# Attention with an image prompt on one core: the image prompt's scores as eight more columns of the last keys' round of maxima

## Chip, cores and metric

One core of a Trainium2 chip runs the whole program. The metric is the device time of one execution in microseconds (us); a result is the median of several executions. All arithmetic is fp32; where a matmul reads fp32r, its operands were split into two parts first, so that the product of the parts keeps fp32's accuracy.

## The reference, cut to what matters

```python
B, S, D, C, HEADS, TEXT, IPT = 8, 512, 320, 512, 20, 1593, 8   # head size 16
text, ip_h = ctx[:, :TEXT], ctx[:, TEXT:]
q = split_heads(x @ w_q)
out_text = softmax(q @ split_heads(text @ w_k).T / 4) @ split_heads(text @ w_v)
out_ip = softmax(q @ split_heads(ip_h @ w_k_ip).T / 4 + mask_ip) @ split_heads(ip_h @ w_v_ip)
out = merge(out_text + out_ip) @ w_out + b_out + x
```

Each of 8 batches has 512 queries and 20 heads of 16. A head attends to 1593 text keys and, in a softmax of its own, to 8 image-prompt (IP) keys under a mask.

## The kernel before

**Groups.** Four heads make a group, so a batch has 5 groups (`NG`) and the program 40. A group's two *stacks* stand at partitions 0 and 64 (`SIDES`): each holds K or Q of two heads in 48 rows, high part, high part and low part of fp32r, so one matmul of depth 48 multiplies exactly. K comes from TensorE in 400-column pieces, is copied from PSUM by ScalarE, split in two parts by GpSimd (`split_k`), stored to HBM by SyncE and loaded into a slot of `k_stack` (a ring of 3 groups).

**Two passes.** Scores are computed twice. First, with queries on the partitions, for their maxima: *rounds* 1 to 16 of a group are three 128x512 matmuls each (`max_tile`, line 699), reduced by VectorE as two banks and then one (lines 1040 and 1042). *Round 0* (`max_rest`, line 710) takes the last 64 keys, of which seven are keys again as padding: 16 matmuls of 64 columns into banks 0 and 1 of `max_bank`, and one reduce of 1024 elements (line 1033). The maxima go through a small matmul with the identity (`negative_piece`, line 618), a ScalarE copy and a DMA into two rows of the Q stack. Second, with keys on the partitions, scores minus maximum (`exp_tile`, line 747, and 751 for the tail), ScalarE's exp (line 935), and the product with V (`pv_tile`, line 763).

**The order.** Everything in the steady state is written out by hand in *visits*: 17 (`v` = 0 to 16) for each group `g`. A visit has two tiles of a round of maxima, three tiles of exp, the round's third tile, mostly one PV tile, and a turn of some other piece from a table, `work_plan` ("Q", "K", "V", "OUT", "IP", the transposes "TA" and "TB" of the IP probabilities, the small products "WA" and "WB"). The rounds run ahead of the exps by a group and three visits: round 0 of group n stands in visit 14 of group n-2, after the exp tiles, and is followed there by the negative piece and a PV tile. Visit 15 begins with two tiles of round 1, which wait for `max_taken`, the semaphore that the last reduce before them counts.

**The image prompt.** `ip_keys` makes K of the IP tokens of all batches once, at the start, twice over two halves of partitions; `own_k` (GpSimd, line 1220) spreads it into a block-diagonal `kip_own` per batch. `ip_piece` (line 559) multiplies a group's whole `q_full` with it, 8 matmuls of 64 columns into the work bank (the trace records each fp32 matmul twice), and `ip_scale` (line 1021) copies them scaled to `s_ip`, two VectorE instructions. The pieces stand at (g, v) = (0, 16), (1, 16), (2, 1), (3, 14), (4, 14), and two at the start. `ip_softmax` has six VectorE steps of a batch, at visits 3, 5, 6, 9, 10, 11 of group 2, with one exp of ScalarE at visit 8.

At the start (`PRO_PLAN`) pieces run without exps; from round 1 of group 0 on each has rounds beside it.

Of the kernel before, what the change touches and what calls it, by code (L numbers as in the profile page):

```python
# [29 lines left out]
VW = DH + 1  # L30

# [36 lines left out]
def work_plan(first, last):  # L68
# [19 lines left out]
    put(0, ("IP", 2), 1, (16, 1))  # L88
# [8 lines left out]
    put(1, ("IP", 3), 1, (16, 1))  # L97
    put(2, ("Q", 4), 3, (0, 3))
    put(2, ("IP", 4), 1, (1, 1))
# [10 lines left out]
    if not last:  # L110
# [11 lines left out]
        put(3, ("IP", 5), 1, (14, 1))  # L122
# [6 lines left out]
        put(4, ("IP", 6), 1, (14, 1))  # L129
# [13 lines left out]
SOFTMAX_AT = (3, 5, 6, 9, 10, 11)  # L143
# [20 lines left out]
PRO_PLAN += [(p, ALL, 0) for p in (("V", 0), ("V", 1), ("KIP",), ("V", 2), ("IP", 0))] + [(("Q", 1), (0, 3, 3), 0)]  # L164
TWO_PLACES = len(PRO_PLAN)
PRO_PLAN += [(("VIP",), ALL, 1), (("IP", 1), ALL, 1)]
PRO_PLAN += [(("V", t), half, 1) for t in range(3, V_FIRST - 1) for half in HALVES]
# [33 lines left out]
def cross_attention(nc, x, x_t, ctx_t, ctx_ip_t, boxes, grid, own_k_rows, own_v_rows, ident, w_q, w_k, w_v, w_k_ip, w_v_ip,  # L201
# [3 lines left out]
    scratch_r = nc.dram_tensor("scratch_r", (GH, S), FP32, kind="Internal").ap()  # L205

    ctx = ExitStack()
    with ctx:
# [14 lines left out]
        own_k_sb = sb("own_k_sb", [128, 8])  # L223
# [17 lines left out]
        k_stack = sb("k_stack", [128, RING, GH // SIDES, KEYS])  # L241
# [18 lines left out]
        kip = sb("kip", [128, NG, B * IPT])  # L260
        vip = sb("vip", [128, 3, B * IPT])
        kip_own = sb("kip_own", [128, NG, 8, IPT])
# [9 lines left out]
        ctx_ip = early[:, 2 * CT * D:2 * CT * D + CT * B * IPT].rearrange("p (c n) -> p c n", c=CT)  # L272

# [49 lines left out]
        kip_ready = sem("kip_ready")  # L323
# [54 lines left out]
        def _(sp):  # L378
# [21 lines left out]
            def load_k(n):  # L400
                sp.wait_ge(k_stored, (n + 1) * 32)
                slot = n % RING
                for side in range(SIDES):
                    for block, part in enumerate(BLOCKS):
                        row = side * SIDE + block * DH
                        sp.dma_start(k_stack[row:row + DH, slot, :, :], k_side(n, side)[part]).then_inc(stack_loaded[slot], 16)
# [9 lines left out]
            def load_first_k(c):  # L416

                sp.wait_ge(k_stored, 32)
                for side in range(SIDES):
                    for block, part in enumerate(BLOCKS):  # L420
                        row = side * SIDE + block * DH
                        sp.dma_start(k_stack[row:row + DH, 0, c, :], k_side(0, side)[part][:, c, :])\
                          .then_inc(stack_loaded[0] if c else head_loaded, 16)

# [42 lines left out]
            sp.wait_ge(stack_cleared, 4)  # L467
# [4 lines left out]
            load_tail(0)  # L472
            store_k(1)
            store_q(1)
            load_k(1)
# [47 lines left out]
        def _(pe):  # L523
# [29 lines left out]
            def ip_piece(g, q_number, kip_count, place=work_bank):  # L553

                pe.wait_ge(work_empty, q_number + 1)
                pe.wait_ge(kip_ready, kip_count)
                for n in range(2):
                    for at, rows in strips(128):
                        last = nc.tensor.matmul(place[at:at + rows, n * 64:(n + 1) * 64],  # L559
                                                q_full[:, n * 128 + at:n * 128 + at + rows],  # L560
                                                kip_own[:, g % NG, :, :].rearrange("p h t -> p (h t)"), start=True, stop=True)
                last.then_inc(work_full, 1)

# [57 lines left out]
            def work(b, piece, turn, first, last):  # L621
# [10 lines left out]
                elif kind == "IP":  # L632
                    ip_piece(piece[1], number(("Q", piece[1])), b + (2 if piece[1] >= NG else 1))
# [41 lines left out]
            def begin_round(n, r):  # L675
# [9 lines left out]
                if taken > 0:  # L685
                    pe.wait_ge(max_taken, taken)

# [80 lines left out]
            def ip_keys(place):  # L768

                for g in range(NG):  # L770
                    for half in range(2):
                        for ct in range(CT):
                            last = nc.tensor.matmul(place[half * GR:(half + 1) * GR, g * 64:(g + 1) * 64],
                                                    wk_ip[:, ct, g * GR:(g + 1) * GR], ctx_ip[:, ct, :],
                                                    start=(ct == 0), stop=(ct == CT - 1))
# [11 lines left out]
            for piece, turn, beside in PRO_PLAN:  # L787
# [17 lines left out]
                elif piece[0] == "IP":  # L805
                    ip_piece(piece[1], PRO_ORDER["Q", piece[1]], 1, place)
# [6 lines left out]
                else:  # L813
                    pe.wait_ge(cleared, 9)
                    pe.wait_ge(consts_loaded, 80)
# [57 lines left out]
        def _(act):  # L873
# [70 lines left out]
            for piece in PRO:  # L944
# [6 lines left out]
                elif piece[0] == "KIP":  # L951
                    act.wait_ge(work_full, number + 1)
                    copy(kip[:, :, :].rearrange("p g n -> p (g n)"), place[:, 0:D]).then_inc(work_empty, 1)
# [4 lines left out]
                elif piece[0] == "IP":  # L958
                    act.wait_ge(work_full, number + 1)
                    src = place[:, 0:128].rearrange("p (n f m) -> p n f m", n=2, f=2)  # L960
                    for half in range(2):
# [395 lines left out]
```

## Time and profile before

| | |
|---|---|
| three runs, median | 1882.86 us (1878.38 to 1886.68) |
| the profiled execution: its time, its span | 1878.19 us, 1876.3 us |
| TensorE busy | 1838.2 us, 98% |
| VectorE busy | 1327.8 us, 71% |
| ScalarE busy | 1202.4 us, 64% |
| GpSimd busy | 379.6 us, 20% |
| DMA share of 16 engines, all queues | 43.9% |

A busy TensorE in this table is an engine with a matmul in flight by the records; a matmul that waits between two others of its kind shows in the timeline only. Times of the profiled execution are given from the start of its span. In the trace "PE" is a matmul and "PEld" its weights' load. The batch in the middle of the span from which most rows below come is the third: its group 1 ends at about 616 us, group 2 at about 662, group 3 at about 706.

### The profile page before, as it was taken

To read this page: it belongs to the slowest core of one execution; us is meant where nothing else is said; L and a number is where in the kernel's file an instruction comes from. 1 tells how busy PE (TensorE), PEld (TensorE's weight loads), DVE (VectorE), ACT (ScalarE), POOL (GpSimd) and SP (SyncE) were. 2 spreads that over 40 slices of the span, in tenths; PEclk is the share of its full clock that TensorE was granted. 3 is DMA by queue.
4 is the path that set the end of the run, shared out by engine and by line. 5 is a ranking of instruction groups with operands and counts; after the bars stand their busy time and mean duration, and the time that the engine had idled before them with its cause. 6 is when DMAs were issued, how large, how long until landed. Compare 5 with 4: busy or idle time off the path is not lost.

```text
span 1876.3 us, 43039 instructions
## 1 busy us (share of the span) xinstructions
PE 1838.2 (98%) x17984; PEld 743.5 (40%) x17984; DVE 1327.8 (71%) x1673; ACT 1202.4 (64%) x2368; POOL 379.6 (20%) x475
## 2 busy tenths in 40 slices
PE   8999999999999999999999999999999999999997
PEld 3333344433444334443443434434344443444332
DVE  5778767686767767677666777667776677676861
ACT  1277666666666666666666666666666666666774
POOL 5112212212112211122211211112121212121000
PEclk9999999999999999999999999999999999999998
DMA  8546334353445444364443643436334363343400
GB/s 233 87 87 157 71 70 101 74 145 71 81 87 135 85 87 86 71 158 84 81 89 70 155 87 70 90 71 168 70 75 83 69 167 71 71 101 67 82 11 23
DMA packets 89011, 175.41 MB, mean 93 GB/s; under 512 B 36197, under 2 KB 60310, under 8 KB 85074
## 3 DMA queue, kind: packets, MB, share of 16 engines
q1 hardware_dynamic: 67826, 131.26, 36.4%
q0 software_dynamic: 18976, 40.10, 6.7%
q8 instruction: 141, 2.31, 0.6%
q10 hardware_dynamic: 2016, 1.31, 0.2%
q14 instruction: 52, 0.43, 0.1%
HBM read 117.57 MB, written 48.82 MB: 89 GB/s over the span
## 4 chain that ended last, share of the span: by engine, by line
PE 93%; DVE 4%; DMA 1%; issue 1%; SPq 1%; ACT 0%; ACTq 0%; POOLq 0%; POOL 0%
PE pv_bank L763 25%; PE max_bank L699 22%; PE work_bank L536 12%; PE work_bank L569 11%; PE exp_bank L747 10%; PE work_bank L585 3%; PE work_bank L547 3%; PE max_bank L710 2%; DVE tile_max L1033 2%; PE exp_bank L751 1%; DVE tile_max L1040 1%; PE work_bank L575 1%; DMA wq<-in_w_q 1%; PE work_bank L596 0%; PE work_bank L559 0%
## 5 line engine op out<-in xcount | busy, mean ns | idle before, releaser
L935 ACT ACTIVATE probs<-exp_bank 128x512 f32<-128x512 f32 x1896 | 995.5, 598 | 436.0 <-PE exp_bank L747 426.0
L1040 DVE TENSOR_REDUCE tile_max<-max_bank 128x2 f32<-128x1024 f32 x632 | 774.1, 1225 | 411.5 <-PE max_bank L699 406.3
L699 PE MATMUL max_bank<-k_stack,q_stack 48*128 48x512 f32 x1896 | 561.3, 464 | 14.4 <-DVE tile_max L1040 11.4
L763 PE MATMUL pv_bank<-probs,v_ones 128*17 128x512 f32 x3840 | 513.3, 599 | 0.1
L1042 DVE TENSOR_REDUCE tile_max<-max_bank 128x1 f32<-128x512 f32 x632 | 429.6, 680 | 0.7 <-PE max_bank L699 0.7
L747 PE MATMUL exp_bank<-q_stack,k_stack 50*128 50x512 f32 x1896 | 409.5, 401 | 2.0 <-DMA q_stack<-neg_rows 1.2
L699 PEld LDWEIGHTS max_bank<-k_stack,q_stack 48*128 48x128 f32 x1896 | 234.1, 184 | 397.9 <-issue 253.4
L536 PE MATMUL work_bank<-ctxt,wk 128*32 128x400 f32 x2528 | 253.5, 506 | 7.7 <-DMA wk<-in_w_k 5.5
L747 PEld LDWEIGHTS exp_bank<-q_stack,k_stack 50*128 50x128 f32 x1896 | 236.4, 187 | 42.5 <-ACT probs L935 29.0
L569 PE MATMUL work_bank<-wv,ctxt 128*32 128x320 f32 x3040 | 246.9, 434 | 0.0
L1233 POOL DMA_DIRECT2D sums<-o_sum x39 | 27.4, 703 | 681.3 <-ACT o_sum L875 681.3
L569 PEld LDWEIGHTS work_bank<-wv,ctxt 128*32 128x32 f32 x3040 | 91.9, 110 | 162.9 <-issue 103.6
L536 PEld LDWEIGHTS work_bank<-ctxt,wk 128*32 128x32 f32 x2528 | 74.9, 110 | 160.8 <-issue 137.6
L763 PEld LDWEIGHTS pv_bank<-probs,v_ones 128*17 128x17 f32 x3840 | 71.0, 95 | 159.9 <-issue 156.0
L1204 POOL TENSOR_TENSOR k_parts<-k_full,zero 128x400 fp32r<-128x400 f32 x80 | 68.6, 857 | 271.4 <-ACT k_full L875 270.9
L875 ACT ACTIVATE v_ones<-work_bank 128x320 f32<-128x320 f32 (+1 forms) x111 | 46.5, 419 | 77.9 <-PE work_bank L569 69.9
L1237 POOL DMA_DIRECT2D scratch_r<-recips x39 | 22.6, 579 | 316.9 <-DVE recips L1060 307.5
L1207 POOL TENSOR_TENSOR k_parts<-k_full,k_parts 128x400 fp32r<-128x400 f32 x80 | 83.3, 1042 | 6.4
L1033 DVE TENSOR_REDUCE tile_max<-max_bank 128x16 f32<-128x1024 f32 x40 | 49.0, 1226 | 37.1 <-PE max_bank L710 37.1
L935 ACT ACTIVATE probs_tail<-exp_bank 128x512 f32<-128x512 f32 x80 | 43.4, 595 | 47.6 <-PE exp_bank L751 47.6
L585 PE MATMUL work_bank<-wout,o_t 128*32 128x320 f32 (+1 forms) x896 | 71.0, 434 | 0.0
L1243 POOL TENSOR_TENSOR o_sum<-o_sum,r_wide 128x512 f32<-128x512 f32 x39 | 50.1, 1285 | 89.8 <-DMA r_wide<-scratch_r 89.8
(125 smaller groups left out, 903.6 us busy)
## 6 DMA issues: line engine op xcount, KB each, us to landing
k_stack<-scratch_k SPq DMA_DIRECT2D x234, 200.0 KB, 6.8
scratch_k<-k_parts SPq DMA_DIRECT2D x80, 400.0 KB, 4.7
ctxt<-in_ctx_t POOLq DMA_DIRECT2D x28, 800.0 KB, 11.2
q_stack<-scratch_q SPq DMA_DIRECT2D x240, 64.0 KB, 2.3
scratch_q<-q_parts SPq DMA_DIRECT2D x80, 128.0 KB, 5.4
r_wide<-scratch_r POOLq DMA_DIRECT2D x39, 256.0 KB, 5.2
xres<-in_x SPq DMA_DIRECT2D x8, 640.0 KB, 6.7
out<-xres SPq DMA_DIRECT2D x32, 160.0 KB, 1.9
```

The lines of the kernel that those rows point to most:

```text
L536: last = nc.tensor.matmul(place[half * GR + at:half * GR + at + rows, 0:CHUNK], wk[:, ct, dims:dims + rows], ctxt[:, ct, keys:keys + CHUNK ...
L569: last = nc.tensor.matmul(place[at:at + rows, 0:D], ctxt[:, ct, key:key + rows], wv[:, ct, :], start=(ct == 0), stop=(ct == CT - 1))
L585: last = nc.tensor.matmul(bank[at:at + rows, :], o_t[0:deep, k, t * 128 + at:t * 128 + at + rows], wout[0:deep, k, :], start=(k == 0), sto ...
L699: nc.tensor.matmul(round_place(n, r)[:, k, :], exact(q_stack[stack, slot, c, t * 128:(t + 1) * 128]), exact(k_stack[stack, slot, c, chunk ...
L747: nc.tensor.matmul(bank[:, :], exact(k_stack[stack, slot, c, kt * 128:(kt + 1) * 128]), exact(q_stack[stack, slot, c, :]), start=True, sto ...
L763: last = nc.tensor.matmul(pv_bank[h * 32:h * 32 + VW, :], v_ones[:, v_slot(b, kt), head * VW:(head + 1) * VW], p, start=(kt == 0), stop=(k ...
L935: nc.scalar.activation(dst, exp_place(group_no, at), ACT.Exp, scale=SCALE).then_inc(probs_ready, 1)
L1033: nc.vector.reduce_max(tile_max[:, :, CHUNKS, :].rearrange("p q s -> p s q"), max_bank[:, 0:SIDES, :].rearrange("p s (q k) -> p s q k", k= ...
L1040: nc.vector.reduce_max(flat[:, at:at + 2], place[:, 0:2, :], AX.X).then_inc(max_taken, 1)
L1042: nc.vector.reduce_max(flat[:, at + 2:at + 3], place[:, 2, :], AX.X).then_inc(max_third_taken, 1)
L1204: nc.gpsimd.tensor_tensor(exact(part[:, 0, :]), k_full[:, c, :], zero[:, :].to_broadcast([128, CHUNK]), ALU.add)\
L1207: nc.gpsimd.tensor_tensor(exact(part[:, 1, :]), k_full[:, c, :], part[:, 0, :], ALU.subtract).then_inc(k_split, 1)
```

## The change

The IP keys become columns of the K stack. `WITH_AGAIN` is 1594, `REST` 58, `WITH_IP` 66, `IN_BANK` 7: of the last keys only 58 stay (one key again instead of seven), the 8 IP keys stand behind them, and round 0 multiplies 66 columns. Seven of the 66-column blocks of a side fit in its bank; the eighth block of both sides goes to bank 2, so side 0 runs one block behind side 1 and the last matmul waits until the first is done (`third_begun`). The IP keys are made on one half of the partitions, split in two parts, stored and loaded to `ip_stack`, and GpSimd places a group's eight columns in its slot (`place_ip`). VectorE takes the maxima in two reduces and copies the IP scores with three more instructions before it counts `max_taken`. The IP pieces, `own_k`, `ip_scale` and the constant `own_k_rows` go; the softmax of the IP scores moves. The diff, cut to its core:

```diff
+WITH_AGAIN = TEXT + 1
+REST = WITH_AGAIN - KEYS // 512 * 512
+WITH_IP = REST + IPT
+IN_BANK = 512 // WITH_IP
...
-    put(0, ("IP", 2), 1, (16, 1))
-    put(1, ("IP", 3), 1, (16, 1))
-    put(2, ("IP", 4), 1, (1, 1))
-        put(3, ("IP", 5), 1, (14, 1))
-        put(4, ("IP", 6), 1, (14, 1))
-SOFTMAX_AT = (3, 5, 6, 9, 10, 11)
+SOFTMAX_AT = ((2, 15), (2, 16), (3, 0), (3, 3), (3, 4), (3, 5))
+IP_EXP_AT = (3, 1)
...
-        k_stack = sb("k_stack", [128, RING, GH // SIDES, KEYS])
+        k_stack = sb("k_stack", [128, RING, GH // SIDES, WITH_AGAIN + IPT])
+        ip_stack = sb("ip_stack", [128, GH // SIDES, NG, B * IPT])
...
+            def store_ip():
+                sp.wait_ge(kip_split, 2)
+                sp.dma_start(scratch_ip.rearrange("a r n -> r a n"), kip_parts).then_inc(kip_stored, 16)
...
@@ begin_round
+                if r == 0:
+                    pe.wait_ge(max_third_taken, max(n, 1) * (ROUNDS - 1))
@@ max_rest
-                for at in range(PAIRS):
-                    c, t = at // QT, at % QT
+                pe.wait_ge(ip_placed, n + 1)
+                for turn in range(PAIRS):
                     for side in range(SIDES):
+                        at = turn if side else (turn - 1) % PAIRS
+                        c, t = at // QT, at % QT
+                        bank, col = (side, at) if at < IN_BANK else (SIDES, side)
                         stack = slice(side * SIDE, side * SIDE + STACK)
-                        mm = nc.tensor.matmul(max_bank[:, side, at * TAIL:(at + 1) * TAIL],
+                        if side and at == IN_BANK:
+                            pe.wait_ge(third_begun, n + 1)
+                        mm = nc.tensor.matmul(max_bank[:, bank, col * WITH_IP:(col + 1) * WITH_IP],
                                               exact(q_stack[stack, slot, c, t * 128:(t + 1) * 128]),
-                                              exact(k_stack[stack, slot, c, CHUNKS * WIDE:KEYS]), start=True, stop=True)
-                        if at == PAIRS - 1:
+                                              exact(k_stack[stack, slot, c, CHUNKS * WIDE:CHUNKS * WIDE + WITH_IP]), start=True, stop=True)
+                        if turn == 0 and side == 0:
+                            mm.then_inc(third_begun, 1)
+                        if turn == PAIRS - 1:
                             mm.then_inc(max_scores, 1)
@@ ip_keys
-                    for half in range(2):
-                        for ct in range(CT):
...
+                    for ct in range(CT):
@@ take_max, round 0
-                    nc.vector.reduce_max(tile_max[:, :, CHUNKS, :].rearrange("p q s -> p s q"),
-                                         max_bank[:, 0:SIDES, :].rearrange("p s (q k) -> p s q k", k=TAIL), AX.X).then_inc(max_taken, 1)
+                    head = max_bank[:, 0:SIDES, 0:IN_BANK * WITH_IP].rearrange("p s (q k) -> p s q k", k=WITH_IP)
+                    end = max_bank[:, SIDES, 0:SIDES * WITH_IP].rearrange("p (s k) -> p s k", k=WITH_IP)
+                    nc.vector.reduce_max(tile_max[:, 0:IN_BANK, CHUNKS, :].rearrange("p q s -> p s q"), head[:, :, :, 0:REST], AX.X)
+                    nc.vector.reduce_max(tile_max[:, IN_BANK, CHUNKS, :], end[:, :, 0:REST], AX.X)
+                    g = n % NG
+                    to = s_ip[:, :, g * GH * IPT:(g + 1) * GH * IPT].rearrange("p t (s c k) -> p c s t k", s=SIDES, c=GH // SIDES)
+                    nc.vector.tensor_scalar(to[:, 0, :, :, :], head[:, :, 0:QT, REST:WITH_IP], SCALE, None, ALU.mult)
+                    nc.vector.tensor_scalar(to[:, 1, :, 0:QT - 1, :], head[:, :, QT:IN_BANK, REST:WITH_IP], SCALE, None, ALU.mult)
+                    nc.vector.tensor_scalar(to[:, 1, :, QT - 1, :], end[:, :, REST:WITH_IP], SCALE, None, ALU.mult).then_inc(max_taken, 1)
@@ GpSimd, once for each group
+            def place_ip(n):
+                if n > RING:
+                    pool.wait_ge(max_taken, (n - RING) * ROUNDS + 1)
+                elif n == RING:
+                    pool.wait_ge(max_taken, ROUNDS)
+                b, g = n // NG, n % NG
+                nc.gpsimd.tensor_tensor(exact(k_stack[:, n % RING, :, WITH_AGAIN:WITH_AGAIN + IPT]), ip_stack[:, :, g, b * IPT:(b + 1) * IPT],
+                                        zero[:, :].unsqueeze(1).to_broadcast([128, GH // SIDES, IPT]), ALU.add).then_inc(ip_placed, 1)
```

Two places in the order of instructions. The first is TensorE at visits 14 and 15 of group 3 in the first batch; line 710 before is line 730 now (round 0), 618 is 631 (the negative piece), 763 is 785 (PV), 559 the IP piece, 699 is 712 (rounds of maxima), 747 is 769 (exp tiles). Before:

```order
357 L747 MATMUL exp_bank<-q_stack,k_stack 128x512 x3
358 L710 MATMUL max_bank<-k_stack,q_stack 128x64 x16
359 L618 MATMUL work_bank<-ident_f,neg_parts 32x128
360 L763 MATMUL pv_bank<-probs,v_ones 17x512 x4
361 L559 MATMUL work_bank<-kip_own,q_full 32x64 x8
362 L699 MATMUL max_bank<-k_stack,q_stack 128x512 x2
```

Now:

```order
351 L769 MATMUL exp_bank<-q_stack,k_stack 128x512 x3
352 L730 MATMUL max_bank<-k_stack,q_stack 128x66 x16
353 L631 MATMUL work_bank<-ident_f,neg_parts 32x128
354 L785 MATMUL pv_bank<-probs,v_ones 17x512 x4
355 L712 MATMUL max_bank<-k_stack,q_stack 128x512 x2
```

The IP piece between PV and the next round's two tiles is gone. The second place is VectorE in the same visits, from the end of round 16 to round 1 (lines 1049, 1052, 1054 are `negative_parts`, 1059, 1062, 1064 now). Before:

```order
220 L1054 TENSOR_TENSOR neg_parts<-neg_max,neg_parts 128x2x8 [waits neg_step]
221 L1033 TENSOR_REDUCE tile_max<-max_bank 128x2x8 [waits max_scores]
222 L1021 TENSOR_SCALAR s_ip<-work_bank 128x2x32 [waits work_full]
223 L1021 TENSOR_SCALAR s_ip<-work_bank 128x2x32
224 L1040 TENSOR_REDUCE tile_max<-max_bank 128x2 [waits max_scores]
```

Now:

```order
235 L1064 TENSOR_TENSOR neg_parts<-neg_max,neg_parts 128x2x8 [waits neg_step]
236 L1038 TENSOR_REDUCE tile_max<-max_bank 128x2x7 [waits max_scores]
237 L1039 TENSOR_REDUCE tile_max<-max_bank 128x2
238 L1042 TENSOR_SCALAR s_ip<-max_bank 128x2x4x8
239 L1043 TENSOR_SCALAR s_ip<-max_bank 128x2x3x8
240 L1044 TENSOR_SCALAR s_ip<-max_bank 128x2x8
241 L1050 TENSOR_REDUCE tile_max<-max_bank 128x2 [waits max_scores]
```

The one reduce of round 0 has become five instructions without a wait between them, of which the last counts `max_taken`; the two copies of the IP piece behind it are gone.

## Rows read from the trace of the kernel before

**Rows 1.** The page: the chain that ended last, by line.
```profile
PE pv_bank L763 25%; PE max_bank L699 22%; PE work_bank L536 12%; PE work_bank L569 11%; PE exp_bank L747 10%; PE work_bank L585 3%; PE work_bank L547 3%; PE max_bank L710 2%; DVE tile_max L1033 2%; PE exp_bank L751 1%; DVE tile_max L1040 1%; PE work_bank L575 1%; DMA wq<-in_w_q 1%; PE work_bank L596 0%; PE work_bank L559 0%
```

**Rows 2.** Windows, one batch: PE, PEld, DVE, ACT, POOL, busy (x), clock, DMA, GB/s.
```profile
460.10:686.80 226.70, 225.81 (x2234) 91.66 (x2238) 162.96 (x206) 150.07 (x296) 46.65 (x59) 1.00 0.45 95
```

**Rows 3.** Timeline, visit 14 of group 3: start, us, engine line [idle before <-releaser].
```profile
697.99 0.68 DVE L1042 TENSOR_REDUCE tile_max<-max_bank 128x1 f32<-128x512 f32 x1
...
698.75 1.12 PEld L710 LDWEIGHTS max_bank<-k_stack,q_stack 48*128 48x128 f32 x16
...
699.92 0.30 PE L618 MATMUL work_bank<-ident_f,neg_parts 128*32 128x128 f32 x1
...
700.02 1.23 DVE L1033 TENSOR_REDUCE tile_max<-max_bank 128x16 f32<-128x1024 f32 x1 [0.60 <-PE max_bank L710]
...
700.80 0.60 PE L559 MATMUL work_bank<-kip_own,q_full 128*32 128x64 f32 x16
...
701.33 0.19 PEld L699 LDWEIGHTS max_bank<-k_stack,q_stack 48*128 48x128 f32 x2
```

**Rows 4.** Timeline, visit 14 of group 2, which has no IP piece there.
```profile
654.31 0.30 PE L618 MATMUL work_bank<-ident_f,neg_parts 128*32 128x128 f32 x1
...
654.42 1.23 DVE L1033 TENSOR_REDUCE tile_max<-max_bank 128x16 f32<-128x1024 f32 x1 [0.83 <-PE max_bank L710]
...
655.70 0.19 PEld L699 LDWEIGHTS max_bank<-k_stack,q_stack 48*128 48x128 f32 x2 [1.04 <-DVE tile_max L1033]
```

**Rows 5.** Lines by form: the reduces and the IP copy (busy us, mean ns).
```profile
L1042 DVE TENSOR_REDUCE tile_max<-max_bank 128x1 f32<-128x512 f32 x632 | 429.6, 680 | 0.7 <-PE max_bank L699 0.7
...
L1033 DVE TENSOR_REDUCE tile_max<-max_bank 128x16 f32<-128x1024 f32 x40 | 49.0, 1226 | 37.1 <-PE max_bank L710 37.1
...
L1021 DVE TENSOR_SCALAR s_ip<-work_bank 128x64 f32<-128x64 f32 x76 | 13.4, 218 | 9.4 <-PE work_bank L559 9.4
```

**Rows 6.** Timeline, VectorE, two reduces with no idle time between them.
```profile
701.90 1.22 DVE L1040 TENSOR_REDUCE tile_max<-max_bank 128x2 f32<-128x1024 f32 x1
703.05 0.68 DVE L1042 TENSOR_REDUCE tile_max<-max_bank 128x1 f32<-128x512 f32 x1
```

**Rows 7.** Timeline, visit 16 of group 1: PV, and the next round behind the IP piece.
```profile
615.03 1.05 PE L763 MATMUL pv_bank<-probs,v_ones 128*17 128x512 f32 x8
...
616.23 0.50 PE L699 MATMUL max_bank<-k_stack,q_stack 48*128 48x512 f32 x2
```

**Rows 8.** Timeline, visit 15 of group 3: PV and directly the next round.
```profile
702.47 1.05 PE L763 MATMUL pv_bank<-probs,v_ones 128*17 128x512 f32 x8
...
703.45 0.82 PE L699 MATMUL max_bank<-k_stack,q_stack 48*128 48x512 f32 x3
```

**Rows 9.** Timeline, visit 1 of group 2: what follows its IP piece.
```profile
621.26 0.18 PEld L699 LDWEIGHTS max_bank<-k_stack,q_stack 48*128 48x128 f32 x2 [0.68 <-DVE tile_max L1040]
```

**Rows 10.** Timeline, the start: IP keys, loads of Q, IP values, first round.
```profile
28.14 3.27 PE L773 MATMUL exp_bank<-probs 128*64 128x64 f32 x80
...
32.08 2.73 SPq L432 DMA_DIRECT2D q_stack<-scratch_q  x6
...
36.26 2.61 PE L781 MATMUL work_bank<-probs 128*128 128x64 f32 x24 [0.50 <-ACT q_full L875]
...
38.80 0.73 PE L699 MATMUL exp_bank<-k_stack,q_stack 48*128 48x512 f32 x3
```

**Rows 11.** Timeline, the start: end of round 16 and round 0 of group 0.
```profile
67.74 0.68 DVE L1042 TENSOR_REDUCE tile_max<-max_bank 128x1 f32<-128x512 f32 x1
...
67.91 1.08 PE L710 MATMUL max_bank<-k_stack,q_stack 48*128 48x64 f32 x16
```

**Rows 12.** Lines by form: a softmax step; timeline, visits 5 and 6 of group 3.
```profile
L1084 DVE TENSOR_TENSOR p_ip<-s_ip,ip_max 128x640 f32<-128x640 f32 x8 | 6.5, 814 | 0.0
...
676.22 1.23 DVE L1040 TENSOR_REDUCE tile_max<-max_bank 128x2 f32<-128x1024 f32 x1 [0.58 <-PE max_bank L699]
...
678.59 1.23 DVE L1040 TENSOR_REDUCE tile_max<-max_bank 128x2 f32<-128x1024 f32 x1 [0.56 <-PE max_bank L699]
```

More of the change, by code:

```diff
@@ L322, in cross_attention @@
         o_packed = sem("o_packed")
-        kip_ready = sem("kip_ready")
+        kip_split = sem("kip_split")
+        kip_stored = sem("kip_stored")
+        ip_stack_loaded = sem("ip_stack_loaded")
+        ip_placed = sem("ip_placed")
+        third_begun = sem("third_begun")
         vip_ready = sem("vip_ready")
@@ L551, in q_piece @@
                     last.then_inc(work_full, 1)
[L553 to L562, printed above, removed]
             def v_piece(t, ct_range, place=work_bank):
@@ L770, in ip_keys @@
                 for g in range(NG):
-                    for half in range(2):
-                        for ct in range(CT):
-                            last = nc.tensor.matmul(place[half * GR:(half + 1) * GR, g * 64:(g + 1) * 64],
-                                                    wk_ip[:, ct, g * GR:(g + 1) * GR], ctx_ip[:, ct, :],
-                                                    start=(ct == 0), stop=(ct == CT - 1))
+                    for ct in range(CT):
+                        last = nc.tensor.matmul(place[0:GR, g * 64:(g + 1) * 64], wk_ip[:, ct, g * GR:(g + 1) * GR], ctx_ip[:, ct, :],
+                                                start=(ct == 0), stop=(ct == CT - 1))
                 last.then_inc(work_full, 1)
@@ L952, in _ @@
                     act.wait_ge(work_full, number + 1)
-                    copy(kip[:, :, :].rearrange("p g n -> p (g n)"), place[:, 0:D]).then_inc(work_empty, 1)
+                    copy(kip, place[0:GR, 0:D]).then_inc(work_empty, 1)
                 elif piece[0] == "VIP":
@@ L957, in _ @@
                     copy(vip[0:64, 2, :], place[0:64, 128:192]).then_inc(work_empty, 1)
[L958 to L961, printed above, removed]
-                        last = nc.scalar.activation(s_ip[:, half * 2:half * 2 + 2, piece[1] * 32:(piece[1] + 1) * 32], src[:, :, half, :],
-                                                    ACT.Copy, scale=SCALE)
-                    last.then_inc(work_empty, 1)
                 elif piece[0] == "V":
@@ L1015, in _ @@
         def _(dve):
-            def ip_scale(g, number):
-                dve.wait_ge(work_full, number + 1)
-                src = work_bank[:, 0:128].rearrange("p (n f m) -> p n f m", n=2, f=2)
-                for half in range(2):
-                    last = nc.vector.tensor_scalar(
-                        s_ip[:, half * 2:half * 2 + 2, (g % NG) * 32:(g % NG + 1) * 32], src[:, :, half, :], SCALE, None, ALU.mult)
-                last.then_inc(work_empty, 1)
             def take_max(n, r):
@@ L1158, in body @@
                                 negative_parts(n)
-                        if g == 2 and v in SOFTMAX_AT:
-                            ip_softmax(b, SOFTMAX_AT.index(v), work_number(b, ("IP", 4), first, last))
+                        if (g, v) in SOFTMAX_AT:
+                            ip_softmax(b, SOFTMAX_AT.index((g, v)))
                         if v == INVERT_AT and group_no:
@@ L1276, in _ @@
             split_q(1, PRO_ORDER["Q", 1])
+            pool.wait_ge(ip_stack_loaded, SIDES * len(BLOCKS) * 16)
+            for n in range(2):
+                place_ip(n)
             for c in range(2):
@@ L1284, in body @@
                     splits = [p for p in SPLITS[g] if not (last and p[1] > 4)]
+                    if group_no + 2 < B * NG:
+                        place_ip(group_no + 2)
                     if group_no:
@@ L1305, in body @@
                             load_ctx(b + 1)
-                    if g == 2 and not last:
-                        pool.wait_ge(work_full, number(("IP", 4)) + 1)
-                        own_k(b + 1)
             batches(body)
```

65 lines of the change are left out of this document (35 added, 30 removed).

## The prediction

> **What bounds the kernel.** I read the chain that ended last first: by line it is nearly all TensorE, with PV, the rounds of maxima and the pieces on top [rows 1]. [...] From that alone every matmul taken away would be time won. But the chain also holds 2% of VectorE's line 1033, the reduce of round 0, and a matmul in flight can be a matmul that the next one doesn't yet follow. So I went to the timeline at the places of the IP pieces, and read from one start to the next.
>
> In visit 14 of group 3 the negative piece starts at 699.92, the reduce of round 0 at 700.02 and runs 1.23 us, to 701.25; the weights of round 1's first tile load at 701.33. The IP piece lies in between, at 700.80 [rows 3]. Group 2 has no IP piece in its visit 14, and looks the same: 654.31, the reduce at 654.42 to 655.65, the weights at 655.70, with line 1033 named as what ended the wait of 1.04 us [rows 4]. From the negative piece to the next round it is 1.41 us with the piece and 1.39 without it. **At this place VectorE sets the time, and two of the five IP pieces of a batch fill a wait.** Round 1 can't start before the reduce is done, whatever TensorE does. The change takes matmuls out of TensorE and puts instructions exactly into this wait.
>
> **Removed: IP pieces at visit 14** (groups 3 and 4). Worth 1.41 - 1.39 = 0.02 us each, taken off below.
>
> **Removed: IP pieces at visit 16** (groups 0 and 1). With the piece it is 616.23 - 615.03 = 1.20 us from PV to the next round [rows 7]; where nothing stands between, 703.45 - 702.47 = 0.98 us [rows 8]. Each is worth 0.22 us; 2 x 8 batches x 0.22 = **-3.5 us**.
>
> **Removed: IP piece at visit 1 of group 2.** The next round's load waits for line 1040, a reduce of the round before, not for this piece [rows 9]. Worth nothing.
>
> **Added: VectorE in round 0.** Now five instructions stand before `max_taken`. Three rows give the cost of one. A reduce of 512 elements takes 680 ns, one of 1024 1226 ns, a scaled copy of 64 elements 218 ns [rows 5]: the first two give (1226 - 680) / 512 = 1.066 ns an element and 134 ns over, the copy 150 ns over. But the next instruction doesn't wait for all of it: line 1042 starts 703.05 - 701.90 = 1.15 us after line 1040, 75 ns before that one's end [rows 6]. So in a row a reduce costs 60 ns and its elements, a copy 75, and the last one its full 150. The elements are 2x7x58 = 812, 2x58 = 116, 64, 48 and 16: 0.926 + 0.184 + 0.143 + 0.126 + 0.167 = **1.55 us** in place of 1.23. The lower bound is the elements alone, 1056 in place of 1024, or 1.26 us; the upper bound has each instruction at its full record, 1.84 us. I take 1.55, since the pair in rows 6 is this very engine, on PSUM, without a wait between.
>
> [...]
>
> From the negative piece to round 1 it is then 0.11 + 1.55 + 0.05 = 1.71 us, 0.32 more than in group 2 [rows 4] and 0.30 more than in group 3 [rows 3], the 0.02 above included. Visits 14 with a round 0 are 38: 24 in groups 0 to 2 and 14 in groups 3 and 4 (the last batch has none there). 24 x 0.32 + 14 x 0.30 = **+11.9 us**. Nothing hides it: everything of visit 15 is queued on TensorE behind this wait, and ScalarE gets its scores later by as much. No later wait gives it back, since TensorE runs without one through most of the next visits.
>
> **Added: TensorE in round 0.** 66 columns in place of 64. [...] The wait for `third_begun` stands at the sixteenth matmul, some 0.9 us behind the first, which is long done. The one for `max_third_taken` asks for line 1042 of round 16: it ends at 697.99 + 0.68 = 698.67, and round 0's first load came at 698.75 anyway [rows 3]. `ip_placed` is counted a whole group earlier. Nothing for these; the cover is the load of 128 columns of weights, and if a wait breaks the row of loads it costs what a load not made early adds: 0.98 us from PV to the next round [rows 8] against 700.80 - 699.92 = 0.88 us from the negative piece with PV to the IP piece [rows 3], 0.10 us.
>
> **Moved: the softmax of the IP scores.** A step is 0.81 us on VectorE [rows 12]. Visits 15, 16 of group 2 and 0 of group 3 are among the longest (they have 2 or 3 turns of V or Q). In visits 3 to 5 of group 3 three steps follow one another; the tightest is visit 5, 678.59 - 676.22 = 2.37 us from reduce to reduce [rows 12], against 1.15 + 0.60 + 0.81 = 2.56 us of work. The 0.2 us by which the next reduce is late is less than the 0.6 us that VectorE idles in an ordinary visit (0.58 and 0.56 [rows 12]), so TensorE shouldn't see it: 0, at most 0.2 x 7 = 1.4 us. The exp on ScalarE moves too, to visit 1 of group 3, which also has room.
>
> **The start.** `ip_keys` halves: 3.2 us [rows 10] become 1.6. The IP piece before Q goes, and the one after round 1: about 0.33 us each as seen from start to start, and Q no longer waits 0.3 us for a copy of V. The first round can't move up by all of it, since it needs the six loads of Q that SyncE issues from 32.08 to 34.81 and that land some 2.3 us later, at about 37.2, where it now starts at 38.80 [rows 10]. So 1.6 us there and 0.35 us behind round 1. Against it: round 0 of group 0 follows directly on round 16, line 1042 of which ends at 67.74 + 0.68 = 68.42, while round 0 began at 67.91 [rows 11]. The new wait holds it 0.55 us. Then the five instructions are passed twice, about 0.3 us each. -1.95 + 0.55 + 0.6 = **-0.8 us**. GpSimd's `split_kip` and SyncE's seven new DMAs stand ahead of the K loads of group 1, wanted only 25 us later; each group's `place_ip` is 16 elements in a queue that idles 80%; the K loads, now in two pieces a row, land visits before they are wanted. All of these at nothing.
>
> **Sum.** -3.5 + 11.9 + 0.3 - 0.8 = **+7.9 us** on the profiled execution's own 1878.2, so 1886.1. That execution is 4.7 us under the median of the three runs shown; against the median, 1882.86 + 7.9 = **1890.8 us**. A change of less than 0.5%, 9.4 us, can hardly be told from none here; this is just under it.
>
> **Rivals.**
> *A, every small instruction costs its whole record.* Round 0's chain on VectorE is 1.84 us, 0.29 more in each of 38 + 2 places: +7.9 + 11.6 = 19.5, **1902 us, slower**. For it: nobody has shown a short instruction right behind another of a different kind. Against: rows 6. It decides from a chain of 1.59 us on, where the sum passes 9.4 us.
> *B, the added waits break TensorE's row of loads.* 0.10 us in each of 38 rounds, +3.8: **1895 us**, slower as well. For it: 698.67 and 698.75 are very close [rows 3], and a load behind a wait isn't made early. Against: the exp tiles have a wait each and follow one another closely.
> *C, the chain is shorter than I think.* At the lower bound, 1.26 us, the stall grows by 0.03 us: 38 x 0.03 - 3.5 + 0.3 - 1.4 = -3.5, **1879 us, no change**.
> *D, TensorE's matmuls count in full.* If each of the 38 pieces in the batches were 0.54 us of path, as the 98% suggest, and the chain lay under PV: -20.5 - 2: **1860 us, faster**. Rows 3 and 4 exclude it almost.
>
> **How the numbers follow.** My own case 0.57, A 0.14, B 0.16, C 0.10, D 0.03. The sum sits 1.5 us under the bound of 0.5%, so of my own case about a quarter falls over it by the runs' own scatter (0.14); A and most of B are over it too. Slower: 0.14 + 0.14 + 0.13 = 0.41; same: 0.43 + 0.03 + 0.10 = 0.56; faster 0.03. The range goes from C with its scatter, 1880, to A, 1903; that leaves out D and the outer half of either end.
>
> **What would show it.** In the profile after: the five VectorE instructions from the first's start to the last's end 1.5 to 1.6 us; from the negative piece to round 1's first load 1.7 us in every group (now 1.39 and 1.41); from PV to the next round at visit 16 of groups 0 and 1 0.98 us; a batch 227.9 us in place of 226.70 (5 x 0.31 + 0.04 - 0.44 = 1.2 more); the first round at about 37.2 us, and round 0 of group 0 right behind the end of round 16's second reduce. I am wrong if round 1 still starts 1.4 us behind the negative piece, if something else than VectorE ends that wait, or if the new row length of 1602 columns in `k_stack` slows the matmuls that read them.

## The result, and the profile after

| | before | after |
|---|---|---|
| median of 22 runs each | 1883.30 us (1878.06 to 1886.68) | 1889.59 us (1884.79 to 1894.86) |
| the profiled execution, its span | 1878.2, 1876.3 | 1890.55, 1888.7 |
| one batch in it, the same reduce to the same reduce, mean of four | 226.70 | 227.58 |
| visit 14, reduce of round 0 to reduce of round 1, groups 0 to 2 / 3 and 4 | 1.85 / 1.88 | 2.14 / 2.14 |
| TensorE instructions, busy | x17984, 98% | x17304, 97% |

The ratio of after to before is 1.0034, with a 95% interval of 1.0025 to 1.0044: **6.3 us slower (4.7 to 8.3)**. The forecast was +7.9, and the result lies 0.34% up, inside the 0.5% that were called no change. One of the twelve executions of e4 below took 9772.89 us and is left out of its comparison.

The page of the changed kernel, against [rows 1]: TensorE still holds the chain that ended last, and round 0's reduce, now line 1038, has its 2% as line 1033 had.

```profile
PE pv_bank L785 25%; PE max_bank L712 20%; PE work_bank L560 12%; PE exp_bank L769 11%; PE work_bank L582 11%; PE work_bank L598 3%; PE work_bank L571 3%; PE max_bank L730 2%; DVE tile_max L1038 2%; PE exp_bank L773 1%; DVE tile_max L1050 1%; PE work_bank L588 1%; PE work_bank L609 0%; DMA ctxt<-in_ctx_t 0%; DVE tile_max L1039 0%
```

One batch against [rows 2], by windows (PE, PEld, DVE, ACT, POOL busy (x), clock, DMA, GB/s): matmuls in flight for 1.2 us less, and the batch 0.9 us longer. The work that was taken out was not what the batch waited for.

```profile
1343.56:1571.10 227.54, 224.59 (x2154) 89.86 (x2155) 162.77 (x215) 150.10 (x297) 46.94 (x63) 1.00 0.45 94
```

Visit 14 of group 2, against [rows 4], is where the time came from. The timeline (start, us, engine line [idle before <-releaser]):

```profile
660.67 0.30 PE L631 MATMUL work_bank<-ident_f,neg_parts 128*32 128x128 f32 x1
...
662.35 0.50 PE L712 MATMUL max_bank<-k_stack,q_stack 48*128 48x512 f32 x2 [0.41 <-DVE s_ip L1044]
...
660.78 1.00 DVE L1038 TENSOR_REDUCE tile_max<-max_bank 128x14 f32<-128x812 f32 x1 [0.83 <-PE max_bank L730]
661.70 0.27 DVE L1039 TENSOR_REDUCE tile_max<-max_bank 128x2 f32<-128x116 f32 x1
661.88 0.21 DVE L1042 TENSOR_SCALAR s_ip<-max_bank 128x64 f32<-128x64 f32 x1
662.01 0.20 DVE L1043 TENSOR_SCALAR s_ip<-max_bank 128x48 f32<-128x48 f32 x1
662.13 0.17 DVE L1044 TENSOR_SCALAR s_ip<-max_bank 128x16 f32<-128x16 f32 x1
...
662.34 0.19 PEld L712 LDWEIGHTS max_bank<-k_stack,q_stack 48*128 48x128 f32 x2 [1.33 <-DVE s_ip L1044]
```

Read it from top to bottom. The five instructions take from 660.78 to 662.30, 1.52 us. Round 1's weights load 0.04 us behind them, 1.67 us behind the negative piece (1.39 before), and the releaser named is the last tiny copy, which is needed only so that bank 2 may be overwritten. TensorE itself idles 0.41 us.

The batches of one trace repeat closely in the steady state (226.65 to 226.72 us before, 227.50 to 227.66 after), so the starts of one reduce per visit, taken in both traces, can be subtracted. Median over six batches, visits with a difference of 0.03 us or more: visit 14 +0.29, +0.29, +0.29 (groups 0 to 2), +0.26, +0.26 (3 and 4); visit 16 of groups 0 and 1 -0.21, -0.22; and two pairs that cancel, -0.16 and +0.16 in visits 1 and 2 of group 2 where the IP piece was, +0.09 and -0.09 in visits 5 and 6 of group 3 where softmax steps now stand. Nothing else moved in these batches.

### The profile page after: what moved, and what is told of

It reads as the page before. It is cut to its first block, busy times and chain, and to the rows that moved or that the text cites. A ratio compares the mean times of both kernels' runs of the same rounds, so it can differ in the third digit from the quotient of the medians.

```text
span 1888.7 us, 41800 instructions
## 1 busy us (share of the span) xinstructions
PE 1835.8 (97%) x17304; PEld 730.8 (39%) x17304; DVE 1327.5 (70%) x1758; ACT 1202.5 (64%) x2364; POOL 383.2 (20%) x508
## 4 chain that ended last, share of the span: by engine, by line
PE 92%; DVE 5%; DMA 1%; issue 1%; SPq 0%; ACT 0%; POOL 0%; POOLq 0%; ACTq 0%
PE pv_bank L785 25%; PE max_bank L712 20%; PE work_bank L560 12%; PE exp_bank L769 11%; PE work_bank L582 11%; PE work_bank L598 3%; PE work_bank L571 3%; PE max_bank L730 2%; DVE tile_max L1038 2%; PE exp_bank L773 1%; DVE tile_max L1050 1%; PE work_bank L588 1%; PE work_bank L609 0%; DMA ctxt<-in_ctx_t 0%; DVE tile_max L1039 0%
## 5 line engine op out<-in xcount | busy, mean ns | idle before, releaser
L893 ACT ACTIVATE k_full<-work_bank 128x400 f32<-128x400 f32 x79 | 39.9, 505 | 46.2 <-PE work_bank L560 46.2
```

The source lines that it names most:

```text
L893: return nc.scalar.activation(dst, src, ACT.Copy)
```

## The experiments

All times are against the kernel before, run on the same chip in the same sitting (its medians there: 1880.36 for e1 to e4, 1880.70 for e5 to e8, 1882.45 for e9 and e10). Intervals are the ratios' 95% ones in us.

**e1: VectorE's chain alone, in the kernel before.**

```diff
-nc.vector.reduce_max(tile_max[:, :, CHUNKS, :]..., max_bank[:, 0:SIDES, :]..., AX.X).then_inc(max_taken, 1)
+turns = max_bank[:, 0:SIDES, :].rearrange("p s (q k) -> p s q k", k=TAIL)
+nc.vector.reduce_max(tile_max[:, 0:7, CHUNKS, :].rearrange("p q s -> p s q"), turns[:, :, 0:7, :], AX.X)
+nc.vector.reduce_max(tile_max[:, 7, CHUNKS, :], turns[:, :, 7, :], AX.X)
+nc.vector.tensor_scalar(to[:, 0, :, :, :], turns[:, :, 0:4, TAIL - 8:TAIL], SCALE, None, ALU.mult)
...
+nc.vector.tensor_scalar(to[:, 1, :, 3, :], turns[:, :, 7, TAIL - 8:TAIL], SCALE, None, ALU.mult).then_inc(max_taken, 1)
```

> The kernel before, with nothing of the change but VectorE's five instructions in round 0: the reduce split into 14 and 2 blocks of 64, and three scaled copies of 64, 48 and 16 elements into a spare tile (an output of no use), the last of them counting max_taken. Everything else, all IP pieces too, stays as before. If the chain on VectorE is what costs (my theory), visit 14 takes 0.28 us more in each of 38 rounds and the two rounds 0 of the prologue as much again: +11 us against before, with 1.5 us from the first reduce's start to the last copy's end. If the cost of the change lies in TensorE (66 columns, three banks, new waits, the longer rows of k_stack), this kernel is no slower than before: within 2 us. If each small instruction took its whole record, it would be +20.

1893.89 us, +13.2 (+9.0 to +17.5). A batch takes 228.57 us, 1.87 more than before, and all of it is in visit 14: +0.39 in groups 0 to 2, +0.36 in 3 and 4.

```profile
662.44 1.09 DVE L1035 TENSOR_REDUCE tile_max<-max_bank 128x14 f32<-128x896 f32 x1 [0.83 <-PE max_bank L711]
663.45 0.28 DVE L1036 TENSOR_REDUCE tile_max<-max_bank 128x2 f32<-128x128 f32 x1
...
663.89 0.16 DVE L1040 TENSOR_SCALAR spare<-max_bank 128x16 f32<-128x16 f32 x1
```

The chain is 1.61 us, not the 1.5 that I expected: I had overlooked that before's blocks have 64 columns where the changed kernel reduces 58, so 96 elements more are read, 0.10 us at the 1.066 ns an element of [rows 5]. With that the two agree: 0.39 - 0.10 = 0.29, which is what visit 14 of the changed kernel shows. VectorE's instructions alone make the whole cost, without one column of TensorE's.

**e2: the IP pieces at visit 14 taken out of the kernel before** (`put(3, ("IP", 5), ...)` and `put(4, ("IP", 6), ...)` deleted, so the scores of the image prompt in these groups are not made).

> The kernel before without its IP pieces at visit 14 of groups 3 and 4 (14 of them; the image prompt's scores of these groups are left out). If they fill a wait for VectorE's reduce (my theory), nothing is won: 14 x 0.02 = -0.3 us, no change. If matmuls count in full on TensorE (rival D), 14 x 0.54 = -7.6 us.

1880.05 us, -0.3 at the medians (-3.9 to +1.7). Visit 14 of groups 3 and 4 is shorter by 0.03 us, a batch by 0.06. Rival D's 7.6 us is outside the interval. Sixteen matmuls that stand in a wait are worth 0.03 us.

**e3: the IP pieces of groups 0 and 1 moved from visit 16 to 14, in the kernel before** (two numbers of `work_plan`).

> The kernel before with the IP pieces of groups 0 and 1 put at visit 14 instead of visit 16; all are still made. By my theory they leave a place where each costs 0.22 us and enter the wait for the reduce, where one costs 0.02: 16 x 0.20 = -3.2 us. If matmuls count in full on TensorE, a place is as good as another: 0.

1879.30 us, -1.1 at the medians (-4.7 to +0.4): the runs alone don't decide it. The trace does: visit 16 is 0.22 us shorter and visit 14 0.04 and 0.03 longer, a batch 226.31 in place of 226.70. The same sixteen matmuls cost 0.22 us in one place and 0.04 in another.

**e4: the changed kernel without the three copies.** `max_taken` is counted by line 1039; the scores are made and not taken out.

> The changed kernel without the three scaled copies in round 0 (the scores of the image prompt are still made by TensorE, but not taken out; the softmax works on zeros). max_taken is then counted by the second reduce. My theory: the chain is 1.20 us in place of 1.52 and the wait at visit 14 goes back to the one of before: 38 x 0.30 + 2 x 0.3 = -12 us against the changed kernel, which is about -6 us against before. If the new cost lies in TensorE's part, the time stays near that of the changed kernel, +4 to +6 against before.

1874.96 us, -5.4 at the medians (-7.9 to -2.8). The chain is 1.19 us, 0.04 less than the single reduce before, and the weights load 1.35 us behind the negative piece (654.61 and 655.96):

```profile
654.61 0.11 PEld L631 LDWEIGHTS work_bank<-ident_f,neg_parts 128*32 128x32 f32 x1
...
655.96 0.19 PEld L712 LDWEIGHTS max_bank<-k_stack,q_stack 48*128 48x128 f32 x2 [1.01 <-DVE tile_max L1039]
```

Everything that the change does on TensorE is still here: 66 columns, three banks, the waits for `third_begun`, `max_third_taken` and `ip_placed`, rows of 1602 columns. Visit 14 takes 1.81 us, less than the 1.85 of before. So none of that costs anything in the steady state, and rival B is out. The second reduce, which exists only since the eight 66-column blocks of a side don't fit in the 512 columns that `max_bank` has for it, costs less than the 96 elements save: 1.19 us for both reduces, 1.23 for the one before.

**e5: the same work, released earlier.** The copies from banks 0 and 1 come right behind their reduce and count `max_taken`; bank 2 follows with a semaphore of its own.

```diff
+nc.vector.tensor_scalar(to[:, 0, :, :, :], head[:, :, 0:QT, REST:WITH_IP], SCALE, None, ALU.mult)
+nc.vector.tensor_scalar(to[:, 1, :, 0:QT - 1, :], head[:, :, QT:IN_BANK, REST:WITH_IP], SCALE, None, ALU.mult).then_inc(max_taken, 1)
 nc.vector.reduce_max(tile_max[:, IN_BANK, CHUNKS, :], end[:, :, 0:REST], AX.X)
-nc.vector.tensor_scalar(to[:, 0, :, :, :], head[:, :, 0:QT, REST:WITH_IP], SCALE, None, ALU.mult)
-nc.vector.tensor_scalar(to[:, 1, :, 0:QT - 1, :], head[:, :, QT:IN_BANK, REST:WITH_IP], SCALE, None, ALU.mult)
-nc.vector.tensor_scalar(to[:, 1, :, QT - 1, :], end[:, :, REST:WITH_IP], SCALE, None, ALU.mult).then_inc(max_taken, 1)
+nc.vector.tensor_scalar(to[:, 1, :, QT - 1, :], end[:, :, REST:WITH_IP], SCALE, None, ALU.mult).then_inc(end_taken, 1)
...
 def begin_third(n, r):
+    if n and r == 1:
+        pe.wait_ge(end_taken, n + 1)
```

> The changed kernel with VectorE's work in round 0 in another order: the reduce of banks 0 and 1, the two copies that read them, and then max_taken; only behind it the reduce and the copy that read bank 2, which count a semaphore of their own that the third tile of round 1 waits for. Nothing is left out. If the chain up to the release is the cost (my theory), it is 0.92 + 0.13 + 0.20 = 1.25 us in place of 1.52: visit 14 back to about before's length, -0.27 x 38 = -10.3 us against the changed kernel, about -4 against before. If TensorE waits for all of VectorE's work in any case (for bank 2, or since the next reduce comes later), the two small instructions behind the release cost as much as before it and the gain is under 2 us.

1876.01 us, -4.7 (-7.0 to -2.6). Visit 14 is 1.87 us, 0.27 less than in the changed kernel in every group. VectorE's rows, and the load that they release:

```profile
652.30 1.00 DVE L1043 TENSOR_REDUCE tile_max<-max_bank 128x14 f32<-128x812 f32 x1 [0.84 <-PE max_bank L735]
653.22 0.21 DVE L1046 TENSOR_SCALAR s_ip<-max_bank 128x64 f32<-128x64 f32 x1
653.35 0.20 DVE L1047 TENSOR_SCALAR s_ip<-max_bank 128x48 f32<-128x48 f32 x1
653.47 0.27 DVE L1048 TENSOR_REDUCE tile_max<-max_bank 128x2 f32<-128x116 f32 x1
653.65 0.16 DVE L1049 TENSOR_SCALAR s_ip<-max_bank 128x16 f32<-128x16 f32 x1
...
653.60 0.19 PEld L715 LDWEIGHTS max_bank<-k_stack,q_stack 48*128 48x128 f32 x2 [1.07 <-DVE s_ip L1047]
```

Look at 653.60: TensorE starts while VectorE is still in its fourth instruction. The third tile, which needs bank 2, comes 0.8 us later. The five instructions are the same as in the changed kernel; three of them stand before the semaphore's count in place of five, and visit 14 is 1.87 us in place of 2.14.

**e6: the wait filled with other work.** In `work_plan` one turn of V or of the output begins at visit 14 of groups 0, 1 and 2, and TA and TB move from 16 to 14:

```diff
-    put(0, ("V", 11), 4, (11, 2), (12, 2))
-    put(0, ("V", 12), 4, (13, 4))
+    put(0, ("V", 11), 4, (11, 1), (12, 1), (13, 2))
+    put(0, ("V", 12), 4, (14, 1), (15, 1), (16, 2))
...
-        put(1, ("OUT", 3), 4, (12, 1), (13, 3))
+        put(1, ("OUT", 3), 4, (14, 1), (15, 1), (16, 2))
...
-        put(2, ("V", 2), 4, (15, 2), (16, 2))
+        put(2, ("V", 2), 4, (14, 1), (15, 2), (16, 1))
...
-        put(3, ("TA",), 4, (16, 4))
-        put(4, ("TB",), 4, (16, 4))
+        put(3, ("TA",), 4, (14, 4))
+        put(4, ("TB",), 4, (14, 4))
```

> The changed kernel with its chain as it is, but with work moved into TensorE's wait at visit 14: one turn of V, or of the output, or the transposes TA and TB from visit 16, stand there in each of the five groups. Nothing is left out. TensorE idles 0.41 us in that wait by the timeline. If it is a wait that takes work for nothing, as the IP pieces of before had it (my theory), each group gets back 0.3 to 0.4 us: 1.7 a batch, -12 us in all against the changed kernel, about -6 against before. If pieces there prolong the wait instead (since the reduce is late by something on TensorE, or ScalarE's copy of the negative row holds the work bank), it is 0 or slower.

1893.80 us, **+13.1 (+11.1 to +16.7): a miss by 19 us**. Visit by visit the filling did what it should: a turn of V costs 0.06 us at visit 14 and 0.54 at 16, TA and TB cost 0.39 in place of 0.87. Groups 0, 2, 3 and 4 win 0.51, 0.48, 0.48 and 0.48 us. Group 1 wins nothing: the output piece costs 1.58 us in visits 14 to 16, but visits 12 and 13, which it left, give back only 0.98, since in visit 13 TensorE now waits for ScalarE's exps. That is 0.60 us lost. And behind group 1 one visit is 2.48 us longer in every batch from the second on. TensorE in visit 13 of group 1, then ScalarE and TensorE in the long visit, by the timeline:

```profile
839.26 1.48 PE L769 MATMUL exp_bank<-q_stack,k_stack 50*128 50x512 f32 x3 [0.40 <-ACT probs L953]
...
853.37 0.60 ACT L893 ACTIVATE o_sum<-pv_bank 128x512 f32<-128x512 f32 x1 [1.75 <-DMA o_t<-o_sum]
...
854.13 3.06 ACT L953 ACTIVATE probs<-exp_bank 128x512 f32<-128x512 f32 x6
...
854.31 0.50 PE L712 MATMUL max_bank<-k_stack,q_stack 48*128 48x512 f32 x2 [0.89 <-DVE tile_max L1050]
854.79 1.47 PE L769 MATMUL exp_bank<-q_stack,k_stack 50*128 50x512 f32 x3
```

The same place in the changed kernel:

```profile
855.15 0.51 PE L712 MATMUL max_bank<-k_stack,q_stack 48*128 48x512 f32 x2 [0.88 <-DVE tile_max L1050]
855.48 0.71 PE L769 MATMUL exp_bank<-q_stack,k_stack 50*128 50x512 f32 x3
```

And the clock in e6, by windows of 1 us (the columns of [rows 2]):

```profile
855.00:856.00 1.00, 1.00 (x4) 0.37 (x3) 1.00 (x1) 1.00 (x3) 0.92 (x2) 1.00 0.83 208
...
857.00:858.00 1.00, 1.00 (x10) 0.29 (x4) 0.02 (x1) 0.18 (x1) 0.67 (x2) 0.50 1.36 115
858.00:859.00 1.00, 1.00 (x8) 0.08 (x2) 0.00 (x0) 0.00 (x0) 0.00 (x0) 0.50 0.63 83
```

The output piece reads `o_t` until visit 16 instead of 13. The next group's output can be packed into `o_t` only then, ScalarE's copy of the PV result waits 1.75 us for that packing, its exps stand queued behind it, and TensorE's three exp tiles, which wait for them, take 1.47 us in place of 0.71. Then its granted clock is 0.50 for 3.4 us. The idle time of 0.89 us before it is not new: the changed kernel has 0.88 us there, and its clock stays at 1.00. A chain over three engines and a DMA that I hadn't followed when I moved the piece.

**e7: early release and filled wait together.**

> The changed kernel with both: the early release of e5 and the moved pieces of e6. By my theory the two share one wait of 0.41 us, so they don't add: the release takes 0.27 of it, the pieces the 0.14 that are left; 38 x 0.41 = -15.6 us against the changed kernel, -9 against before. If they were independent the sum of both, -22, would come.

1897.91 us, +17.2 (+13.9 to +19.4): a miss by the same piece. What it was for shows in the trace all the same: visit 14 is 2.19 and 2.52 us, to the hundredth as in e6. Where other work fills the wait the release brings nothing, so the two share one wait. The trace also splits the 2.48 us: in two of its batches the clock doesn't fall behind group 1, and there the long visit takes 3.40 and 3.42 us, against 2.54 in the changed kernel and 5.02 in e6. So about 0.9 us are the late exps, and 1.6 us the low clock. By the medians e7 is 4 us slower than e6; its steady batches don't show why, and that stays open.

**e8: the wait filled in the kernel before**: e3, and V 2 at (14, 1), (15, 2), (16, 1).

> The kernel before with its own wait at visit 14 filled in every group: the IP pieces of groups 0 and 1 from visit 16 to 14 as in e3, and one turn of V in group 2; groups 3 and 4 have an IP piece there already. It tells whether the changed scheme is worth anything once both kernels use the wait. My theory: 16 x 0.20 for the pieces and 7 x 0.2 for V, -4.6 us against before, and so 4 us slower than e7. If TensorE's work counts wherever it stands, 0.

1877.71 us, -3.0 at the medians (-5.8 to -1.7). In group 2 visit 14 grows by 0.34 and visit 16 shrinks by 0.54: the turn of V takes all that was idle there (0.20 us; in the changed kernel it was 0.48). A batch takes 226.10 us. Whether other pieces would fill this kernel's wait better was not tried.

**e9: e6 with group 1's output piece back at visits 12 and 13.**

> e6 with the output piece of group 1 left where the changed kernel has it (visits 12 and 13); the moved pieces of groups 0, 2, 3 and 4 stay at visit 14. In e6 these four took 0.51, 0.49, 0.49 and 0.49 us from each batch, and group 1 lost 2.4 us behind them: DMA o_t<-o_sum came late for ScalarE's copy of o_sum, and the granted clock fell for 3.4 us. If that one piece was the cause (my theory), a batch is 227.58 - 1.98 = 225.6 us, and the kernel -14 us against the changed one, about -8 against before. If filling the wait brings the low clock by itself, the stretch at 0.5 stays in each batch, with the time near e6, +13 against before.

1872.93 us, -8.8 at the ratio (-12.2 to -5.6). A batch is 225.69 us; groups 0, 2, 3 and 4 keep their gains, the 0.60 and the 2.48 us of e6 are gone, and so is the low clock at that place, though TensorE idles 0.88 us there, as in the changed kernel. So the one piece was the cause, and the filled wait alone did not bring the clock down here: it is 1.00 at that place in each batch.

```profile
651.23 0.92 PE L582 MATMUL work_bank<-wv,ctxt 128*32 128x320 f32 x8
652.08 0.50 PE L712 MATMUL max_bank<-k_stack,q_stack 48*128 48x512 f32 x2
```

The turn of V starts at 651.23, and round 1 at 652.08 with no idle time before it, where the changed kernel idled 0.41 us.

**e10: e9 with the early release.**

> e9 with the early release of e5. e6 and e7 had the same length of visit 14 (2.19 and 2.52 us), so where the wait is filled the release adds nothing; it counts in group 1 alone, and in the last batch: 227.58 - 1.98 - 0.27 = 225.3 us a batch, 8 x 0.27 + 0.8 = 3 us less than e9, about -11 against before. If release and filling were independent it would be 13 us less than e9 (as in e5 against the changed kernel).

1870.15 us, **-11.7 against before (-14.7 to -8.8)**. A batch is 225.41 us, 0.28 less than in e9, all of it in visit 14 of group 1 (-0.27 to 1.87 us). This version computes everything and has the lowest median of all that ran. Its interval overlaps that of e9, so between these two it is the trace that decides. Against e8, before with its wait filled too, a batch is 0.69 us shorter.

## Why the prediction was right

The sum, term by term, with what the traces show in its place:

| term | forecast | shown |
|---|---|---|
| IP pieces at visit 16 | 16 x 0.22 = -3.5 | 16 x 0.21 = -3.4 |
| VectorE's chain at visit 14 | 24 x 0.32 + 14 x 0.30 = +11.9 | 24 x 0.29 + 14 x 0.255 = +10.5 |
| 66 columns, and all waits added | +0.3 | 0 (e4) |
| softmax, steady state | 0 | 0 |
| softmax, last batch, without the low clock | not looked at | -2.5 and +2.5 |
| the start | -0.8 | about -0.9 |
| **sum** | **+7.9** | **+6.2; runs: +6.3** |

*What bounds it.* "At this place VectorE sets the time, and two of the five IP pieces of a batch fill a wait": e2 measured 0.03 us for such a piece (forecast 0.02), e3 0.22 and 0.04 for the same piece in two places, e1 the chain alone. This was the step that made the sign right; TensorE's 98% would have given rival D.

*The chain.* Forecast 1.55 us, shown 1.52; from the negative piece to round 1 forecast 1.71, shown 1.67. The term is 1.4 us too large in all, since each small instruction in the middle came 0.01 us sooner than the 75 ns and its elements that I had taken from two large reduces. The bounds, 1.26 and 1.84, were both far off.

*Rival A.* The starts 660.78, 661.70, 661.88, 662.01, 662.13 lie 0.92, 0.18, 0.13 and 0.12 us apart, while the records last 1.00, 0.27, 0.21 and 0.20: each instruction starts 0.08 to 0.09 us before the one ahead of it ends, down to one of 48 elements. With whole records the chain would be 1.00 + 0.27 + 0.21 + 0.20 + 0.17 = 1.85 us; it is 1.52. The rows of the forecast had this overlap for two large reduces only; these five show it for the small instructions.

*The 66 columns.* No run shows the forecast's +0.3 us; it was an estimate of mine. e4 has the 66 columns, and its visit 14 takes 1.81 us against 1.85 before; at the start sixteen matmuls of 66 columns take the 1.08 us (67.79 below) that sixteen of 64 took [rows 11].

*Rival B.* The load of round 0's weights stayed in its row; e4 has every added wait and a shorter visit 14 than before. *Rival C* asked for a chain of 1.26 us. It came true only in e4 and e5, where the chain up to the release is 1.19 and 1.25 us; both are faster than before.

*The start.* Here the two profiles mislead. After's first round began at 38.67 us, 0.13 before that of before, and not at 37.2; TensorE had waited 0.78 us there for the load of Q. But the start differs from one execution to the next: over all twelve profiled executions, the first reduce of the rounds began at 39.44 to 41.15 us in the five of kernels that start like before (mean 40.1) and at 37.82 to 39.31 in the seven of those that start like after (mean 38.7), 1.4 us sooner; the forecast was 1.6. Behind it, up to the body, executions without a stretch of low clock there agree to 0.1 us: after loses 0.5 us, made of 0.6 won until round 16 (forecast 0.35), 0.6 for the wait before round 0 of group 0 (0.55) and two chains of 0.3 and 0.2 (0.3 each). The one price that was off was `ip_keys`, whose forty records took from 28.65 to the next piece at 31.13, 2.5 us in place of the 1.6 that half of [rows 10] would be.

```profile
28.65 2.54 PE L794 MATMUL exp_bank<-probs 128*64 128x64 f32 x40
31.13 2.36 PE L582 MATMUL work_bank<-wv,ctxt 128*32 128x320 f32 x32
...
67.01 0.68 DVE L1052 TENSOR_REDUCE tile_max<-max_bank 128x1 f32<-128x512 f32 x1
...
67.79 1.08 PE L730 MATMUL max_bank<-k_stack,q_stack 48*128 48x66 f32 x16 [0.55 <-issue]
```

The rows at 67 are the new wait: round 0's first matmul at 67.79, right behind 67.01 + 0.68 = 67.69.

*What I left out.* The last batch has no K and V pieces of a next one, so its visits come down to VectorE's own two reduces (the shortest in before 1.84 and 1.85 us from reduce to reduce), and a softmax step lengthens each by about 0.5 us. In group 2 five visits lost 0.61, 0.49, 0.61, 0.28 and 0.52 us when the steps left; in group 3 the six steps brought 0.34, 0.08, 0.57, 0.57, 0.42 and 0.55 back. It cancels, but not by any argument of mine. And the low clock comes on top. In two visits of group 3 TensorE now idles longer, 1.37 and 1.25 us where before it was 0.80 and 0.88, and in the profiled execution the granted clock is 0.50 for 3.4 us behind each:

```profile
1802.95 0.50 PE L712 MATMUL max_bank<-k_stack,q_stack 48*128 48x512 f32 x2 [1.37 <-DVE tile_max L1050]
...
1813.02 0.50 PE L712 MATMUL max_bank<-k_stack,q_stack 48*128 48x512 f32 x2 [1.25 <-DVE tile_max L1050]
```

Against executions without it these visits are 2.4 us longer. Five of the six others with the moved softmax have one such stretch behind one of the two, worth 0.8 to 1.0 us. The sum of +6.2 holds none of this; with it, it would be +7.0 to +8.6, of which most still lies in the measured interval of 4.7 to 8.3. That the table comes within 0.1 us of the medians is partly luck.

*The profiled pair.* It differs by 12.4 us, twice the medians' 6.3. The last batch's low clock is 2.4 us of this, and some 4 us are a stretch of low clock in the first batch, in group 1's last visits, where in that batch no output pieces stand:

```profile
160.00:170.00 10.00, 10.00 (x53) 2.88 (x55) 4.98 (x6) 4.57 (x9) 0.00 (x0) 0.57 0.71 167
```

The profiled execution of before happened to have none of it; those of e1 to e8, built on either kernel, all had some. A single pair of profiles gives the mechanism, not the size.

## What to carry to other kernels

Before taking an instruction out of the busiest engine, look at what ends its wait at that place: here sixteen matmuls were worth 0.03 us in one visit and 0.22 two visits later. Work added to the other engine counted here only as far as it stood before the semaphore that the busy engine waits for (visit 14 took 2.14 us with five instructions before it and 1.87 with three), so release first what is waited for, and give the rest a semaphore of its own. Work moved into a wait must be followed to everything that reads or frees its buffers: one output piece moved by two visits cost 3 us in each batch, 0.6 in its own group and 2.5 by way of a DMA, ScalarE and the clock.

## What was not expected of the hardware

In e6 the granted clock fell to 0.50 about 2 us after an idle time of 0.88 us on TensorE, and stayed there for 3.4 us, in each batch from the second on. The idle time alone doesn't decide it: the changed kernel and e9 idle 0.88 us at the same place in each batch, and there the clock stays at 1.00; e7 idles 0.88 us in seven batches, and the clock fell behind it in five. What e6 and e7 add there are the exp tiles of 1.47 us. In ten of the twelve profiled executions it also fell in the first batch, around 150 to 170 us. Near 1800 us all seven profiled executions with the moved softmax show the low clock, and one of the five others; in six of the seven a stretch follows one of the two longer idle times above. What decides it, these runs don't tell, and the softmax was not moved alone.

Forty matmul records that all write the same half of the partitions (`ip_keys`) took 62 ns each, where eighty, eight for one half and then eight for the other, took 40 ns each [rows 10]. Taking one of two halves away gave back 0.7 us of 3.2, not half of it. The cause is open.
